# Chunks 0 and 1 of the output projection moved into the score stream, and the score lead-in moved into the first block

## What is computed

```
Q = proj([Wq x, conv3(Wq x)]); K likewise; V = Wv x
tau, delta = sigmoid(pointwise(gelu(depthwise3(x))))
scores = (Q K^T / 4) * tau[q] + delta[k]
a = softmax(scores) V;  x = layernorm(x + Wo a + bo)
x = layernorm(x + quant(x) quant(W)^T + bf)
```

## Time and profile before

| what | value |
|---|---|
| median of three runs | 1696.35 us |
| profiled execution | 1700.33 us, span 1698.5 us, mean granted clock 0.981 |
| PE busy | 1642.5 us (97%) |
| DVE busy | 1538.2 us (91%) |
| ACT busy | 1322.7 us (78%) |
| chain that ended last | PE 62%, DVE 21% |
| maxima, line 218 | 1024 of 1223 ns |

### The profile page before, as it was taken

How to read it: one execution, slowest core, us unless ns; L and a number is a source line. 1 busy time by engine, 2 the same in 40 slices (tenths; PEclk the granted TensorE clock), 3 DMA queues, 4 the chain that set the end, 5 groups by cost and what they waited for, 6 DMA issues and landing times.

```text
span 1698.5 us, 33654 instructions
## 1 busy us (share of the span) xinstructions
PE 1642.5 (97%) x13972; PEld 745.1 (44%) x13978; DVE 1538.2 (91%) x1638; ACT 1322.7 (78%) x2389; POOL 74.6 (4%) x133
## 2 busy tenths in 40 slices
PE   8999989999999999999999999999999999998977
PEld 7677754333333333333333333333333333334466
DVE  5588977999999999999999999999999999985797
ACT  3688723888888888888888888888888888885534
POOL 3000003000000000000000000000000000001110
PEclk9899997999999999999999999999999999999998
DMA  3376436000600060006002400322050000002232
GB/s 111 91 191 171 123 91 95 9 8 8 76 16 8 8 84 8 8 9 83 8 14 30 66 8 8 51 44 61 29 71 21 8 8 8 8 8 86 82 101 75
DMA packets 46961, 84.73 MB, mean 50 GB/s; under 512 B 9116, under 2 KB 21020, under 8 KB 44092
## 3 DMA queue, kind: packets, MB, share of 16 engines
q1 hardware_dynamic: 44952, 82.49, 22.6%
q10 hardware_dynamic: 1856, 0.09, 0.1%
HBM read 51.36 MB, written 30.67 MB: 48 GB/s over the span
## 4 chain that ended last, share of the span: by engine, by line
PE 62%; DVE 21%; ACT 1%; issue 1%; ACTq 0%; POOL 0%; DVEq 0%
PE ps L846 26%; PE ps L833 20%; DVE mx L218 17%; PE ps L208 11%; PE ps L869 1%; PE ps L914 1%; PE ps L867 1%; PE ps L820 0%; DVE stats L1059 0%; DVE work L1094 0%; DVE work L1093 0%; ACT e L989 0%; DVE work L1085 0%; DVE small L1080 0%; DVE scr L1089 0%
## 5 line engine op out<-in xcount | busy, mean ns | idle before, releaser
L218 DVE TENSOR_REDUCE mx<-ps 128x2 f32<-128x1024 f32 x1024 | 1230.4, 1223 | 60.6 <-PE ps L208 51.2
L989 ACT ACTIVATE e<-ps 128x512 f32<-128x512 f32 x2048 | 1110.3, 596 | 210.5 <-PE ps L833 170.4
L846 PE MATMUL ps<-e,v_grp 128*32 128x256 f32 x8192 | 657.7, 393 | 0.2 <-issue 0.2
L833 PE MATMUL ps<-q,k 52*128 52x512 f32 x2048 | 525.3, 499 | 4.0 <-ACT e L989 4.0
L208 PE MATMUL ps<-k,q 50*128 50x512 f32 x2048 | 420.8, 404 | 11.1 <-DVE mx L218 6.5
L833 PEld LDWEIGHTS ps<-q,k 52*128 52x128 f32 x2048 | 199.4, 184 | 430.8 <-ACT e L989 400.0
L846 PEld LDWEIGHTS ps<-e,v_grp 128*32 128x32 f32 x8192 | 162.1, 108 | 359.2 <-issue 202.4
L208 PEld LDWEIGHTS ps<-k,q 50*128 50x128 f32 x2048 | 198.9, 188 | 39.7 <-DVE mx L218 31.0
L608 PE MATMUL ps<-x_p,m_p 128*128 128x512 f32 x576 | 143.1, 405 | 0.0
L608 PEld LDWEIGHTS ps<-x_p,m_p 128*128 128x128 f32 x576 | 109.1, 193 | 31.0 <-issue 6.5
L440 DVE SCALAR_TENSOR_TENSOR hid<-x_c,dw_w,hid 128x512 f32<-128x512 f32 x128 | 88.5, 746 | 13.2 <-ACT hid L382 13.2
(11 more groups left out here) (127 smaller groups left out, 621.8 us busy)
## 6 DMA issues: line engine op xcount, KB each, us to landing
k<-k_parts SPq DMA_DIRECT2D x42, 256.0 KB
q<-q_parts SPq DMA_DIRECT2D x42, 256.0 KB
k_parts<-k_sp SPq DMA_DIRECT2D x16, 512.0 KB, 5.1
q_parts<-q_sp SPq DMA_DIRECT2D x16, 512.0 KB, 4.6
att<-ev SPq DMA_DIRECT2D x32, 256.0 KB
x_c<-in_x_t SPq DMA_DIRECT2D x8, 514.0 KB, 6.4
tau_r<-tau_rows SPq DMA_DIRECT2D x16, 256.0 KB
x_in<-in_x SPq DMA_DIRECT2D x8, 512.0 KB, 3.7
```

Source lines behind the costliest of these rows:

```text
L218: nc.vector.tensor_reduce(mx[:, j % 2, :, jh, qt, kc], ps[:, b0:b0 + 2, :], AX.X, ALU.max).then_inc(s_free, 1)
L833: nc.tensor.matmul(ps[:, st_bank(n), :], k_set[r, g % 2, jh, kt * P:(kt + 1) * P], q_set[r, g % 2, jh, lo:lo + CH], start=True, stop=True) ...
L846: last = nc.tensor.matmul(ps[32 * h:32 * (h + 1), 0, PVW * part:PVW * (part + 1)], v_grp[:, kt, h, :], e[:, x % E_BUFS, h * CH + PVW * par ...
L989: nc.scalar.activation(e[:, x % E_BUFS, h * CH:(h + 1) * CH], ps[:, st_bank(n), :], ACT.Exp).then_inc(e_ready, 1)
```

## The change

It does five things. (1) `PRE_STEP` takes 42 items in the first block instead of 28: 5 in chunk 2, 6 each in chunks 3 to 6, and 13 in chunk 7, there one after every six matmuls of `project`. Units of iteration 0 are now ordered by key chunk, so that early ones need only early loads. The row maxima of iteration 0, their transposition and `rows_store(0)` come in chunk 7. (2) The opening of the second block with its `WARM` matmuls is gone; items 42 to 44 are added to iteration 0, which so issues 36. (3) In the first chunk, `values(0, 1)` has a bank of its own and DVE takes `v_bias(0, 0)` after the next chunk's first taps. (4) Eight items "o" stand in the stream at units 5, 13, 21 and 29 of iterations 27 and 28: a quarter of the output projection of chunk 0 or 1 each, which DVE copies to SBUF. The loads of chunks 2 and 3 and POOL's `normalise` of chunks 0 to 3 move from the tail to iterations 24 to 30. (5) `PROJECT_AT` places chunks 2, 3 and 4 in the last iterations, and the loop behind them projects chunk n + 5 after `linear(n)`; `ROOT_AT` and the sums' loads and stores follow.

```diff
+        O_AT = {(27 + n, 8 * a + 5): ("o", n, a) for n in range(2) for a in range(TT)}
+            if j == 0:
+                return u % (HH * TT) // HH, u % HH, u // (HH * TT)
+            if j == 0 and (qt, jh) == (0, 0):
+                pe.wait_ge(group_loaded, 16 * GROUP_DMAS * (kc + 1))
-        V_BANK, TD_BANK = 2, 3
+        v_bank = lambda n, v: 5 if (n, v) == (0, 1) else 2
-        PRE_STEP = {4: (0, 0, 0, 0, 0, 0, 2), 5: (0, 0, 1, 1, 1, 1, 1), 6: (0, 0, 1, 1, 1, 1, 1), 7: (2, 2, 2, 2, 2, 2, 4)}
+        PRE_STEP = {2: ONE_EACH(6, 9, 10, 13, 14)} | {n: ONE_EACH(5, 6, 9, 10, 13, 14) for n in range(3, 7)} | {7: [1] * 13 + [0, 0]}
...
-                sp.wait_ge(k_stored, 16 * CT * NCHUNK)
-                sp.wait_ge(q_stored, 16 * CT * NCHUNK)
-                sp.wait_ge(d_stored, 16 * NCHUNK)
-                sp.wait_ge(group_loaded, loads_of(1))
+                nc.scalar.activation(warm_exp[:], eps_col[:], ACT.Exp)
...
-                    if n == 0:
-                        v_bias(n, 0)
                     if more:
                         tap(n + 1, 0, range(4))
...
                         side_bias_of(0, 1)
+                        v_bias(n, 0)
...
-                    for s in range(PRE, lead_in):
-                        s_item(s)
-                        for m in range(WARM):
...
-                    issued = lead_in
+                    issued = PRE
                     for i in range(NIT):
-                        due = min(PER, len(items) - issued)
-                        slots = SLOTS if due == PER else SLOTS * 3 // 4
+                        goal = items.index((i + 2, LEAD)) if i + 2 < NIT else len(items) - 1
+                        due = goal - issued
+                        slots = SLOTS * 3 // 4 if i == NIT - 2 else SLOTS
...
+                                if i == NIT - 2 and 2 * k + jh == slots:
+                                    s_item(len(items) - 1)
...
+            PROJECT_AT = {x0 + a: (n, a) for n, x0 in ((2, LAST - 2), (3, LAST + 2), (4, LAST + 11)) for a in range(TT)}
+            ROOT_AT = {LAST - 1: (0, 1), LAST + 5: (2,), LAST + 9: (3,)}
...
                     for n in range(NCHUNK):
                         transposed(n)
-                        if n + EARLY < NCHUNK:
+                        linear(n)
+                        if n + EARLY + 1 < NCHUNK:
                             for a in range(TT):
-                                project(n + EARLY, a)
-                        linear(n)
+                                project(n + EARLY + 1, a)
```

More of the change, by code:

```diff
@@ L532, in pre_max @@
                 def pre_max(n, place):
-                    for s in pre_at.get((n, place), ()):
+                    for s in (s for p in DVE_PLACES[place] for s in pre_at.get((n, p), ())):
+                        j, u = items[s]
+                        if u == "rows":
+                            rows_copy(dve, s)
+                            continue
                         max_unit(dve, s)
+                        if u == UNITS - 1:
+                            row_maxima(dve, s)
                 for n in range(NCHUNK):
                     more = n + 1 < NCHUNK
-                    if n == 0:
-                        v_bias(n, 0)
                     if more:
@@ L603, in beta, with project @@
                     last.then_inc(beta_full, 1)
-                def project(n, side, o, done):
+                def project(n, side, o, done, place):
                     terms = [(c, tap, k) for c in range(CT) for tap in range(TAPS) for k in THREE]
                     for m, (c, tap, (kw, kx_)) in enumerate(terms):
-                        last = nc.tensor.matmul(ps[:, o, :], m_p[:, kw, side, c, tap, P * o:P * (o + 1)], x_p[:, n % 2, kx_, c, tap:tap + CH],
-                                                start=(m == 0), stop=(m == len(terms) - 1))
-                    last.then_inc(done, 1)
+                        mm = nc.tensor.matmul(ps[:, o, :], m_p[:, kw, side, c, tap, P * o:P * (o + 1)], x_p[:, n % 2, kx_, c, tap:tap + CH],
+                                              start=(m == 0), stop=(m == len(terms) - 1))
+                        if m == len(terms) - 1:
+                            mm.then_inc(done, 1)
+                        if m % 6 == 5:
+                            pre_scores(n, place + m // 6)
                 def values(n, v):
-                    if 2 * n + v > 0:
+                    if n > 0:
                         pe.wait_ge(v_evac, 2 * n + v)
@@ L633, in pre_scores @@
                     for s in pre_at.get((n, place), ()):
-                        s_unit(pe, s)
+                        if items[s][1] == "rows":
+                            rows_turn(pe, s)
+                        else:
+                            s_unit(pe, s)
                 beta(1, 0)
@@ L907, in linear @@
                                 last.then_inc(f_full, 1)
-                    for s in range(PRE, lead_in):
-                        s_item(s)
-                        for m in range(WARM):
-                            for half in range(2):
-                                r = rows_of(half, K_S)
-                                nc.tensor.matmul(ps[:, st_bank(half), :], q_set[r, 0, 0, 0:P], k_set[r, 0, 0, 0:CH], start=True, stop=True)
                     for x in range(AHEAD):
@@ L1195, in _ @@
                                 refill(g + 1, c)
-                    for n in range(NCHUNK):
+                    for n in range(EARLY, NCHUNK):
                         normalise(n)
```

283 lines of the change are left out of this document (167 added, 116 removed).

## The result

The changed kernel takes 1709.11 us (median of 7 runs, 1700.29 to 1709.63) against 1696.35 us for the kernel before (7 runs beside it): ratio 1.0051, 95% interval 1.0027 to 1.0075 (the quotient of the two medians alone is 1.0075). It is slower by about half a per cent, where 1681 was forecast. The profiled execution took 1709.26 us, its span is 1707.5 us (before 1698.5), and its mean granted clock 0.973 (before 0.981).

The account below looks back on a forecast made before the run. PE sets the stream's pace, DVE follows closely and bounds the end. Front -13.6, projection blocks +12.9 and stretch to chunk 4's start -15.0 sum to -15.7 us, giving about 1681 us; range 1672 to 1691.

Parts of the forecast that it names:

- The 75.6 us behind it stay: the same DVE chain.: Tail, from chunk 4's start on DVE to the end: unchanged at 75.6 us.
- The eight blocks: Projection blocks put in the stream: 1.51 us of PE each plus 0.1 for displaced units, +12.9 us in all.
- The clock: Behind P: a 13.8 us stretch at 1.2 GHz as before, 6.4 slow half-tiles, 5.8 us lost.
- The last item of the stream: End of the stream: one half-tile later but without the 1.22 us wait for POOL, net 0.
- P: First value matmul of the second block, 279.64 before: forecast to move by -16.9 us.
- The front as a whole: First block, seam, opening and three more units in iteration 0: stream forecast 13.6 us earlier.
- s5: Fifth `scales`, chunk 4's start on DVE in the tail: forecast 79.5 us behind S, 94.5 before.
- S: Last item of the stream, at 1528.44 before: forecast at 1527.7.
- Early clock: Rival at iteration 0's start: one short slow stretch and no second, 5.8 us less, 1675; chance 0.17.
- DVE bind in the first block: Rival: DVE bounds first block and double half-tiles, 4 us each, and tail gains 4 less, 1693; chance 0.09.
- The clock stays low: Rival in the second block: all of iteration 0 at 1.2 GHz, +23 us, 1704; chance 0.04.
- The tail does not do what it says: Rival in the tail: chunk 4's chain waits for something else, projections moved for nothing, 1690; chance 0.10.

Follow-up runs that it names:

- e1: Changed kernel with transposed(n + 1) ahead of the projection of chunk n + 5 in PE's last loop: 0.9952 of the kernel before.
- e2: Changed kernel with ACT's finish(n - 1), including its square root, ahead of turn(n) in the last loop: 1.0012 of the kernel before.
- e3: Kernel before with only the front part of the change, keeping its old last iterations and tail: 0.9922 of the kernel before.
- e5: Changed kernel with the transposition ahead of the projection, and two DVE rounding instructions left out for chunks 0 to 3: 0.9961 of the kernel before.
- e8: e1 with chunk 4 drawn into the early part and linear(2) with its statistics drawn forward: 1681.44 us, 0.9892 of the kernel before.
- e4: Changed kernel with 12 unused matmuls behind PE's last projection in the first block: 1.0034 of the kernel before.
- e6: Front part of the change with the old tail, and two DVE rounding instructions left out for chunks 0 to 3: 0.9941 of the kernel before.
- e9: Kernel before with only the changed stream, SP, POOL and tail, keeping its old front: 1.0085 of the kernel before.

## Why the prediction was wrong

**The failed step** is the last sentence on the tail: "The 75.6 us behind it stay: the same DVE chain." It measured 92.5, 16.9 us more, and this alone uses up the whole gain of 15.7 that was forecast. DVE's chain was the same; the ring that feeds it was not. Before, PE transposed chunk n and then projected chunk n + 4; the change puts `linear(n)` ahead of the projection, so the next transposition comes behind it. The diff showed this in four lines. They have no term in the sum, since I took DVE to be the bound there and did not follow what its mid-chain `scale_shift(1, m)` waits for: root, turn, transposition, projection, norm. e1 and e2 cut the ring at two links, and both remove DVE's idle spans. Some 5.4 us of the loss, by the estimate above, came with the slow clock that followed PE's own waits in the ring.

**Terms of the right mechanism and the wrong size.** The eight blocks: 12.9 forecast (bounds 11.2 to 17), 16.8 between e3 and e1. From the third row copy to the last, the seven kernels with blocks and the new front take 1190.1 to 1193.9 us and the three without 1175.9 to 1176.8, a mean difference of 15.1. 8 x 1.85 = 14.8 is the block itself, since the displaced unit costs a half-tile of its own 0.59 and not 0.1; another 1.2 is in the last interval between row copies, 42.77 us in e1 and 41.54 in e3. The clock: 5.8 us lost were assumed. In the profiled execution 24.88 / 2.16 = 11.5 half-tiles were slow, 10.4 us lost. Seven other executions with the same code at that place (e1 to e3, e5 to e8) go in 55.4 to 58.3 us from the first row copy to the second, where this one took 62.4, so some 4 us of it are not in the others; its time is that of the median execution, 1709.11, all the same. The last item of the stream: the 1.22 us wait for POOL was taken to go, but PE waits 1.24 us for POOL there (the transposition at 1534.74).

**Right:** first chunk -4.2 (forecast -3.5); first block +12.6 from chunk 1 to the last projection (+12.0); end of it 3.4 us (4.0); opening 3.8 us (4.2); P -18.0 (-16.9). The front as a whole, 13.6 forecast, is 0.78% or 13 us in e3, with an interval of 5 to 19.

**Right in part by luck:** s5 at S + 79.9 (S + 79.5). From the last row transposition iteration 31 took 74.0 us and not 71.4, and what follows it 6.3 and not 8.1, so two errors nearly cancel. The prediction had no term for the 23.8 us of slow clock in iteration 31: a half-tile takes 1.73 us there (1539.52 to 1541.25) and 1.12 at full clock (two from 1576.22 to 1578.46).

The sum, in the profiled execution: P -18.0, clock and iteration 0 +6.1 up to the third row copy, blocks and last iterations +18.2, S to s5 -14.2, s5 to the end +16.9: +9.0.

**The rivals.** "Early clock" did not come, nor did DVE bind in the first block (no chunk over 27.5 us). "The clock stays low" had its mechanism, a longer slow stretch, but less than half its price, and it is not the cause: e4, with a slow stretch of 6.7 us, kept the fault of the tail and stayed at 1.0034. "The tail does not do what it says" was nearest: it had the place and ended at 1690, as it took the loss of the gain for the worst case. None had the case that happened, a chain that is slower than before; hence 0.05 for slower. One line of the section on what would prove me wrong did name it: an end more than 77 us behind the fifth `scales`. Another, a wait of PE in the stream for POOL, came too, but at the size that it had before.

## What to carry to other kernels

When an instruction list is reordered in a loop shared by three engines, follow the whole ring once: for the engine that bounds, take the waits in the middle of its chain, and for each go back through every in-order queue, asking what now stands ahead. A stage that "is bound by DVE" holds its time only while everything that feeds it keeps its slack. Which engine bounds a stage is told in one run by taking time out of the suspected one (e5, e6). And where the same engine bounds both the tail and the stream, as PE did here up to the fifth `scales`, moving its work from one to the other wins nothing: S came 16.8 us later and s5 15.9 us nearer to it.

## What the hardware showed that was not expected

The clock stayed at its lower level under full load. Behind P, PE was busy 24.88 of 24.88 us at clock 0.50, that is 1.2 GHz. With the same code at that place the slow stretch lasted 13.8 us before and none in e9, and between 10 and 27 us in eight traces with the new front. The Trainium skill, "TensorE: Matmul & The Clock Gate", part 1, says that activity releases the half rate; this trace does not agree for that stretch.

A multiplication on GpSimd (POOL) lengthens an instruction of VectorE that works in SBUF at the same time. In the timeline after:

```profile
1623.03 2.40 POOL L1242 TENSOR_TENSOR v_all<-v_all 128x1024 f32<-128x1024 f32 x1 [30.41 <-DMA v_all<-rz_rows]
1623.06 2.92 DVE L1158 TENSOR_SCALAR work<-work 128x1024 f32<-128x1024 f32 x1
...
1626.02 0.69 DVE L1159 TENSOR_SCALAR scr<-work 128x1024 int32<-128x1024 int32 x1
```

DVE's `tensor_scalar` over 128x1024 takes 2.92 us beside POOL's `tensor_tensor`, and its neighbour of the same size 0.69. A `tensor_tensor` of DVE went from 1.22 to 3.08 us beside one in e1 (at 1564.14), and a `tensor_scalar` of 128x32 from 0.18 to 2.40 after (at 1572.44). These three cost DVE 1.9 to 2.2 us each. DVE's maxima, which read PSUM, are not held up: beside POOL's multiplication at 1509.67, moved into the stream by the change, three take 3.70 us, 1.23 each. The Trainium skill, "GPSIMD Engine Reference", section 8, says that the two engines share their SBUF interfaces, and names instructions of VectorE in a 2-port mode or with two SBUF inputs. The trace agrees for the `tensor_tensor`, which has two; in which mode a `tensor_scalar` ran, no run here shows.
